# Attention's end: three of the last unit's four tiles by squares and transfers, in place of two

## The chip, the cores and the metric

The kernel runs on one core of a Trainium2 chip. A core has five engines that work side by side and are kept in step by semaphores only: PE (matmul), ACT, DVE, POOL and SP, which does nothing here but issue transfers. The metric is the time of one execution on the device in microseconds, the median of three: 640.15 (639.71 to 640.76).

## The reference, cut to what matters

4096 tokens of 128 values go through three steps, each with a layer norm in front: a mixture-of-experts feed-forward (8 experts, the best 2 per token, and a shared one), an attention over 4096 stored keys and values, and the same feed-forward again.

```python
x = x + 0.5 * ffn(layernorm(x))
x = x + attn(layernorm(x))      # the part that counts here
x = x + 0.5 * ffn(layernorm(x))

q = h @ Wq.T + bq
scores = einsum('bshd,hmd->bshm', q, memory_keys) / sqrt(128)
probs = softmax(scores)
out = einsum('bshm,hmd->bshd', probs, memory_values) @ Wo.T + bo
```

Everything is in 32-bit floats; the kernel splits the operands of the large products into a high and a low part and adds three products.

## The kernel before, in words

The tokens form 8 groups of 512 (four tiles of 128). The attention takes a group against half of the keys (2048) at a time: a **unit**. There are 16 units, 0 to 15; `LAST` is 15.

A unit has 8 half tiles of scores. For each of them PE multiplies (L1488 to L1490), DVE takes the maximum (L1205), and ACT takes the exponentials. The product with the values needs these exponentials with the keys on the partitions, so each 128x128 block has to be turned. There are two ways:

- **By PE** (an "own" tile): ACT writes the exponentials in plain rows (L852), PE transposes each block into PSUM (L1508), ACT copies the high part (`own_high`, L802), and DVE takes the low part (`own_low`, L1193).
- **By squares and transfers** (a "moved" tile): ACT writes the exponentials as 32x32 squares (L843), DVE turns each square in place (`transpose_squares`, L1200, twice per tile), and transfers carry the squares to their place in `probsT` (`move_strip`, L383). ACT then takes the high part (`moved_high`, L818) and POOL the low part (`moved_low`, L608).

`moved_tiles(w)` says how many of the four tiles go the second way: 3 (`MOVED`) in units 1 to 14, and 2 in unit 0 and unit 15.

The keys of a unit are taken in 8 **pairs** of blocks (`UP`). For each pair there are the transposes of the own tiles on PE (`transpose_pair`), `own_high` and `own_low` of what they wrote, `moved_high` and `moved_low` of the moved tiles, and six products with the values (`values`, L1529 to L1531). One PSUM bank, `TB`, holds the transposes, so those of the next pair wait until `own_low` has read the last ones (`p_lo_done`). PE has the order: transposes of pair r+2, then values of pair r.

What follows the order of the work:

- Every engine has its own order, written out by one loop over half steps H = 8u + h. In the last unit's tail (H from 127) ACT does in each half step: `own_high` of a pair, then `moved_high` of the pair behind it. DVE does `own_low` and pieces of other work: maxima, the normalizing L989, and the 16 steps of the routing for the second feed-forward (`route_group`, four per half step, between two `own_low`).
- Pair 0 of a unit can't have its `moved_high` before that unit's transfers are down (`moved[0]`, `moved[1]`): `moved[0]` counts the first two tiles, `moved[1]` the third.
- The transfers of a unit from 3 on are in two batches (`BATCHES`). SP issues batch 0, two tiles in 16 issues of 128 KB, after the squares of both tiles. Then it issues batch 1, the third tile, in 12 issues of 64 KB; the last 4 of batch 1 are issued by ACT, at h = 7, behind the unit's last exponentials (L918 to L924). SP works its list in order.
- In the tail ACT also copies for the second feed-forward: L796 waits for nothing but PE's transposes and stands between `moved_high` of the last unit's pair 0 and its `own_high`. PE's gate products (L1282) wait for that copy and stand in front of the transposes of pair 1.
- POOL has, between the `moved_low` of the last unit's pairs 2 and 3, the addition of a block (L624, L629) and three small operations (L510, L511, L513). The copy L867 on ACT, which stands in front of `own_high` of pair 3, waits for the addition.

Of the kernel before, what the change touches and what calls it, by code (L numbers as in the profile page):

```python
# [35 lines left out]
UNITS = 2 * GROUPS  # L36
# [5 lines left out]
LAST = UNITS - 1  # L42


MOVED = 3
# [11 lines left out]
HALVES = 2 * GT  # L57
# [3 lines left out]
SINGLE = 2  # L61
# [42 lines left out]
def macaron_kernel(nc: bass.Bass, x, wup, wdown, gate_w, expert_bias, shared_up, shared_down,  # L104
                   wq, bq, wo, bo, keys_values, out):
    with ExitStack() as ctx:
# [186 lines left out]
        def wait(eng, s, n):  # L293

            if not isinstance(n, int) or n > 0:
                eng.wait_ge(s, n)
# [31 lines left out]
        def early_logits(i):  # L328

            return (TB, banks[:, 3, :], banks[:, 1, :])[i][:, 0:P]  # L330

        def moved_tiles(w):

            return 2 if w in (0, LAST) else MOVED

        def moved_pair(w, m):

# [20 lines left out]

        def moves(k, units):

            later = max(0, (units if k == 0 else min(units, LAST)) - SINGLE - 1)
            return MOVE * ((min(units, 1) if k == 0 else 0) + later)

        def squares_of(units):
            return 2 * sum(moved_tiles(w) for w in range(units))
# [15 lines left out]
        def move_strip(eng, u, k, tile, count, b, i):  # L381
            done = single[u - 1][tile] if 0 < u <= SINGLE else moved[k]
            eng.dma_start(*strip(u, tile, count, b, i)).then_inc(done, 16)  # L383
# [7 lines left out]
        def pair_at(H):  # L391

            return pairs_until(H) if pairs_until(H + 1) > pairs_until(H) else None

        def projection_at(H):

            w = H // HALVES - 2
            if w < 0 or w >= LAST:
                return None
            return w if H % HALVES == (FIRST_LAG if w == 0 else LAG + 1) else None  # L400
# [269 lines left out]
        def _(act):  # L670
# [25 lines left out]
            def exp_logits(G, logits):  # L696

                act.wait_ge(logits_done, G + 1)
                if G >= 2:
                    act.wait_ge(expz_turned, route_event(G - 2) + 1)  # L700
                act.activation(early_rows if G == GROUPS else expz_rows[:, G % 2, :], logits, ACT.Exp, scale=-1.0).then_inc(expz_done, 1)
# [16 lines left out]
            def copy_wbc(G, bank):  # L718
                act.wait_ge(wbc_done, G + 1)
                wait(act, weighted, (G - 1) * SLOTS)  # L720

                act.activation(wbc[:, G % 2, :].rearrange("p (t a q) -> p t a q", t=GT, a=GT),
                               bank.rearrange("p (a t q) -> p t a q", a=GT, t=GT), ACT.Copy).then_inc(wbc_copied, 1)
# [51 lines left out]
            def copy_xT_for_q(g, bank):  # L775

                act.wait_ge(xT_done, g + 1 + ATTENTION_LN)
                wait(act, q_projected, g)
                act.wait_ge(shared_up_done, GROUPS - AHEAD)
                act.wait_ge(xTb_done, GROUPS - AHEAD)  # L780
                act.activation(xq[:, :], bank, ACT.Copy).then_inc(xT_copied, 1)

            def q_high(g, bank):

                act.wait_ge(q_projected, g + 1)
                wait(act, scores_done, BANKS * GT * 2 * (g - 1))
                act.activation(q_hi[:, g % 2, :], bank, ACT.Identity, bias=bq_scaled[:, 0:1]).then_inc(q_hi_done, 1)

            def early_copy(i, bank):

                if i == 0:
                    act.wait_ge(q_projected, GROUPS)
                else:
                    act.wait_ge(probsT_done, UP * LAST)
                act.wait_ge(xT_done, SECOND_LN + i + 1)
                act.activation(xT[i], bank, ACT.Copy).then_inc(xT_copied, 1)  # L796

            def own_high(ring):

                act.wait_ge(probsT_done, ring + 1)  # L800
                wait(act, pv_done, 2 * (ring - HI_RING + 1))
                act.activation(own_part(p_hi, ring), own_squares(ring), ACT.Copy).then_inc(p_hi_done, 1)  # L802
# [54 lines left out]
            def copy_oT(w):  # L857

                act.wait_ge(pv_done, (w + 1) * KC)
                wait(act, out_proj_done, w)  # L860
                act.activation(oT[:, :], OB, ACT.Copy).then_inc(oT_copied, 1)

            def copy_y(w):

                act.wait_ge(out_proj_done, w + 1)
                wait(act, block_added, w)
                act.activation(y[:, :, :].rearrange("p t d -> p (t d)"), projection_bank(w), ACT.Copy  # L867
                               ).then_inc(y_copied, 1)

            def shift_exponentials(g):  # L870

                act.wait_ge(shift_done, g + 1)
                act.activation(shift_exp[:, :, :].rearrange("p b t -> p (b t)"),
                               shift[:, :, :].rearrange("p b t -> p (b t)"), ACT.Exp).then_inc(shift_exp_done, 1)
# [4 lines left out]
            for u in range(UNITS + 2):  # L879
                g = u // 2  # L880
                prepares = u % 2 == 1 and u < LAST
                for h in range(HALVES):
                    H = u * HALVES + h
                    w = projection_at(H + 3)
                    if u <= LAST and w:
                        copy_oT(w)
                    if projection_at(H + 2) == 0:
                        copy_oT(0)
                    if u == LAST + 2 and h == LAG - 2:
                        copy_oT(LAST)  # L890
                    if u == LAST + 1 and h == 3:
                        early_copy(1, banks[:, 1, :])
                    if u == LAST + 1 and h == 5:
                        exp_logits(GROUPS + 1, early_logits(1))
                        early_copy(2, banks[:, 0, :])
                    if u == LAST + 1 and h == 7:
                        exp_logits(GROUPS + 2, early_logits(2))
                    if u == LAST + 2 and h == 3:
                        copy_wbc(GROUPS, banks[:, 2, :])

                    ring = pair_at(H + 3)
                    if ring is not None:
                        own_high(ring)

                    if u > LAST and w is not None:
                        copy_oT(w)
                    if u < UNITS:
                        exponentials(u, h // 2, h % 2)
                    if u == 0 and h == 6:
                        for done in moved_first[:QUADS * QUADS // 2]:  # L910
                            act.wait_ge(done, 16)
                    of, at_h = divmod(H - 4, HALVES)
                    if 1 <= of <= SINGLE and at_h in (0, 2, 4):
                        tile = at_h // 2
                        wait(act, moved_lo_done, UP * (of - 1))
                        act.wait_ge(squares_done, squares_of(of) + 2 * (tile + 1))
                        if of == 1 and tile == MOVED - 1:
                            act.wait_ge(probsT_done, UP)  # L918
                        for i in range(QUADS):
                            move_strip(act, of, 0, tile, 1, QUADS - 1, i)  # L920
                    if SINGLE < u < LAST and h == HALVES - 1:
                        wait(act, moved_lo_done, UP * (u - 1))
                        act.wait_ge(squares_done, squares_of(u) + 2 * MOVED)
                        for i in range(QUADS):  # L924
                            move_strip(act, u, 1, MOVED - 1, 1, QUADS - 1, i)
                    if prepares and h == Q_HALF - 2:
                        copy_xT_for_q(g + 1, TB)
                    if prepares and h == Q_HALF - 1:
                        q_high(g + 1, TB)
                    if u == LAST and h == Q_HALF - 2:  # L930
                        early_copy(0, TB)
                    if u == LAST and h == Q_HALF - 1:
                        exp_logits(GROUPS, early_logits(0))

                    ring = pair_at(H + 4)
                    if ring == 1:
                        moved_high(0)
                    if ring:
                        moved_high(ring)
                    w = projection_at(H + 2)  # L940
                    if w is not None:
                        copy_y(w)
                    if 2 <= u and u % 2 == 0 and h == 1:
                        shift_exponentials(g - 1)
# [722 lines left out]
```

## Time and profile before

| | |
|---|---|
| median of three runs | 640.15 us (639.71 to 640.76) |
| the profiled execution | 640.2 us, span 638.4 us |
| busy share of the span | PE 94%, DVE 82%, ACT 71%, POOL 65% |
| granted PE clock | full in all 40 slices |
| chain that ended last | PE 65%, DVE 24%, issue 4%, ACT 3% |
| `moved_low` (L608) | 128 of them, 226.9 us of POOL |
| squares (L1200) | 92 of them, 113.5 us of DVE |

The rows shown further down are of these kinds. A row of the chain of waits gives the start, the time in the chain and the work that the end was waiting for. A row of the timeline gives the start, the busy time, engine, line, operation and shapes; x2 stands for two in a row, and the brackets say how long the engine stood idle before and what released it. SPq and ACTq are the queues in which these engines issue transfers. A row of a group gives count, total busy time and the mean in ns. The attention's last scores are at about 514 us, its last products with the values end at about 550.6, and then the second feed-forward runs to the end.

### The profile page before, as it was taken

To read this page: it belongs to the slowest core of one execution; us is meant where nothing else is said; L and a number is where in the kernel's file an instruction comes from. 1 tells how busy PE (TensorE), PEld (TensorE's weight loads), DVE (VectorE), ACT (ScalarE), POOL (GpSimd) and SP (SyncE) were. 2 spreads that over 40 slices of the span, in tenths; PEclk is the share of its full clock that TensorE was granted. 3 is DMA by queue.
4 is the path that set the end of the run, shared out by engine and by line. 5 is a ranking of instruction groups with operands and counts; after the bars stand their busy time and mean duration, and the time that the engine had idled before them with its cause. 6 is when DMAs were issued, how large, how long until landed. Compare 5 with 4: busy or idle time off the path is not lost.

```text
span 638.4 us, 10666 instructions
## 1 busy us (share of the span) xinstructions
PE 597.5 (94%) x3508; PEld 443.3 (69%) x3508; DVE 525.7 (82%) x915; ACT 455.0 (71%) x756; POOL 414.7 (65%) x482
## 2 busy tenths in 40 slices
PE   6798989889899999999999999999999998988987
PEld 2456666567687787777778777787787766655655
DVE  5989886988978978978988897887888858688775
ACT  3577776566777767777777777776876775578886
POOL 3977880564486875966767687596677787645420
PEclk9999999999999999999999999999999999999999
DMA  8012110425447265363643726527355350000000
GB/s 309 13 34 67 37 64 1 128 62 129 112 100 173 55 169 116 84 166 85 147 113 86 178 69 150 128 71 171 91 136 118 82 134 0 1 2 34 35 33 34
DMA packets 36118, 59.28 MB, mean 93 GB/s; under 512 B 9312, under 2 KB 9952, under 8 KB 35936
## 3 DMA queue, kind: packets, MB, share of 16 engines
q1 hardware_dynamic: 31808, 52.82, 32.7%
q10 hardware_dynamic: 3744, 4.74, 2.9%
q0 software_dynamic: 512, 1.05, 0.6%
q8 instruction: 28, 0.46, 0.3%
q14 instruction: 26, 0.21, 0.1%
HBM read 8.25 MB, written 2.10 MB: 16 GB/s over the span
## 4 chain that ended last, share of the span: by engine, by line
PE 65%; DVE 24%; issue 4%; ACT 3%; SPq 1%; DMA 1%; POOL 1%; ACTq 0%; DVEq 0%; POOLq 0%
PE banks L1488 8%; PE banks L1489 7%; PE banks L1490 7%; PE banks L1529 7%; PE banks L1531 7%; PE banks L1530 7%; DVE probsT L1096 6%; PE banks L1508 4%; DVE bank_max L1205 4%; PE banks L1345 4%; DVE E L1200 3%; PE banks L1330 3%; PE banks L1539 2%; PE banks L1361 2%; PE banks L1358 2%
## 5 line engine op out<-in xcount | busy, mean ns | idle before, releaser
L608 POOL TENSOR_TENSOR p_lo<-probsT,p_hi 128x768 fp32r<-128x768 f32 (+1 forms) x128 | 226.9, 1776 | 120.8 <-ACT p_hi L818 120.2
L1205 DVE TENSOR_REDUCE bank_max<-banks 128x1 f32<-128x1024 f32 x128 | 155.9, 1219 | 30.6 <-PE banks L1490 29.8
L818 ACT ACTIVATE p_hi<-probsT 128x768 fp32r<-128x768 f32 (+1 forms) x128 | 104.4, 816 | 29.0 <-PE banks L1531 26.6
L1096 DVE SCALAR_TENSOR_TENSOR probsT<-banks,E 128x1024 bf16<-128x1024 f32 x80 | 95.4, 1216 | 24.7 <-PE banks L1330 24.7
L1488 PE MATMUL banks<-kv_lo,q_parts 128*128 128x512 f32 x256 | 111.6, 436 | 4.1 <-ACT E L843 1.9
L1200 DVE STREAM_TRANSPOSE E<-E 128x1024 f32<-128x1024 f32 x92 | 113.5, 1234 | 0.3 <-ACT E L843 0.2
L843 ACT ACTIVATE E<-banks,neg_max 128x1024 f32<-128x1024 f32 x92 | 102.4, 1113 | 9.7 <-DVE neg_max L1211 8.0
L1529 PE MATMUL banks<-p_hi,kv_lo 128*128 128x512 f32 x256 | 107.7, 421 | 1.7 <-issue 1.7
L716 ACT ACTIVATE probsT<-probsT 128x1024 bf16<-128x1024 bf16 x96 | 92.4, 981 | 16.7 <-DVE probsT L1096 12.4
L1530 PE MATMUL banks<-p_lo,kv_hi 128*128 128x512 f32 x256 | 102.3, 399 | 0.0
L1531 PE MATMUL banks<-p_hi,kv_hi 128*128 128x512 f32 x256 | 102.3, 399 | 0.0
L1489 PE MATMUL banks<-kv_hi,q_parts 128*128 128x512 f32 x256 | 101.4, 396 | 0.0
L1490 PE MATMUL banks<-kv_hi,q_parts 128*128 128x512 f32 x256 | 101.0, 394 | 0.0
L802 ACT ACTIVATE p_hi<-banks 128x256 fp32r<-128x256 f32 (+1 forms) x128 | 52.3, 408 | 62.4 <-PE banks L1508 62.1
L1193 DVE TENSOR_TENSOR p_lo<-banks,p_hi 128x256 fp32r<-128x256 f32 (+1 forms) x128 | 56.1, 438 | 32.4 <-ACT p_hi L802 32.1
L1345 PEld LDWEIGHTS banks<-wdown_b,probsT 128*128 128x128 bf16 x704 | 42.5, 98 | 30.8 <-ACT probsT L716 21.7
L1345 PE MATMUL banks<-wdown_b,probsT 128*128 128x128 bf16 x704 | 52.8, 220 | 7.9 <-ACT probsT L716 7.9
L1529 PEld LDWEIGHTS banks<-p_hi,kv_lo 128*128 128x128 f32 x256 | 48.3, 189 | 14.0 <-issue 4.0
L1330 PE MATMUL banks<-E,wup_b 128*128 128x512 bf16 x176 | 50.8, 381 | 7.3 <-DVE probsT L1096 6.3
L1488 PEld LDWEIGHTS banks<-kv_lo,q_parts 128*128 128x128 f32 x256 | 48.3, 189 | 12.8 <-ACT E L843 3.4
L1531 PEld LDWEIGHTS banks<-p_hi,kv_hi 128*128 128x128 f32 x256 | 48.1, 188 | 12.3
L1530 PEld LDWEIGHTS banks<-p_lo,kv_hi 128*128 128x128 f32 x256 | 48.2, 188 | 11.7 <-issue 1.7
(133 smaller groups left out, 928.3 us busy)
## 6 DMA issues: line engine op xcount, KB each, us to landing
probsT<-E SPq DMA_DIRECT2D x208, 128.0 KB, 2.4
probsT<-E SPq DMA_DIRECT2D x232, 64.0 KB, 2.0
probsT<-E ACTq DMA_DIRECT2D x72, 64.0 KB, 2.1
E<-in_keys_values SPq DMA_DIRECT2D x8, 512.0 KB, 3.6
out<-X SPq DMA_DIRECT2D x8, 256.0 KB, 2.0
X<-in_x SPq DMA_DIRECT2D x1, 1280.0 KB, 9.3
probsT<-E POOLq DMA_DIRECT2D x16, 64.0 KB, 2.4
X<-in_x SPq DMA_DIRECT2D x3, 256.0 KB, 5.5
```

Of the source, the lines that this page charges most:

```text
L608: pool.tensor_tensor(moved_part(p_lo, ring), moved_pair(ring // UP, ring % UP), moved_part(p_hi, ring).bitcast(fp32), ALU.subtract).then_i ...
L818: act.activation(moved_part(p_hi, ring), moved_pair(ring // UP, ring % UP), ACT.Copy).then_inc(moved_hi_done, 1)
L1096: dve.scalar_tensor_tensor(hidden[:, k, :, :], up_banks[PAIR_BANK[k]], 0.0, spread.unsqueeze(1).to_broadcast([P, 2, N]), ALU.max, ALU.mult ...
L1200: dve.transpose(half, half).then_inc(squares_done, 1)
L1205: dve.tensor_reduce(bank_max[:, i % 2, h:h + 1], score_pair(u, i, h).rearrange("p b n -> p (b n)"), AX.X, ALU.max).then_inc(bank_max_done, 1)
L1345: last = pe.matmul(result_banks[G % 2][:, t * D:(t + 1) * D], hidden[:, k, c % 2, t * P:(t + 1) * P], wdown_b[:, c, :], start=(c == 0 and ...
L1488: pe.matmul(bank, qh, kl, start=True, stop=False)
L1489: pe.matmul(bank, ql, kh, start=False, stop=False)
L1490: pe.matmul(bank, qh, kh, start=False, stop=True).then_inc(scores_done, 1)
L1529: pe.matmul(OB, vl, hi, start=(c == 0), stop=False)
L1530: pe.matmul(OB, vh, lo, start=False, stop=False)
L1531: pe.matmul(OB, vh, hi, start=False, stop=(c == KC - 1)).then_inc(pv_done, 1)
```

## The change

Unit 15 now has three moved tiles, like the units in front of it. Its third tile gets two more squares on DVE, 12 more issues on SP and 4 more on ACT; its PE transposes fall from four to two per pair, `own_high` and `own_low` from 512 to 256 columns, and `moved_high` and `moved_low` grow from 512 to 768. The thresholds of `moved[1]` follow.

```diff
         def moved_tiles(w):
 
-            return 2 if w in (0, LAST) else MOVED
+            return 2 if w == 0 else MOVED
...
         def moves(k, units):
 
-            later = max(0, (units if k == 0 else min(units, LAST)) - SINGLE - 1)
+            later = max(0, units - SINGLE - 1)
...
-                    if SINGLE < u < LAST and h == HALVES - 1:
+                    if SINGLE < u < UNITS and h == HALVES - 1:
                         wait(act, moved_lo_done, UP * (u - 1))
                         act.wait_ge(squares_done, squares_of(u) + 2 * MOVED)
                         for i in range(QUADS):
```

On SP, at the end of its list: the two batches of unit 14, batch 0 of unit 15 and the stores of the output before

```order
L383 DMA probsT<-E 32x2x512 x16
L383 DMA probsT<-E 32x512 x12
L383 DMA probsT<-E 32x2x512 x16
L462 DMA out<-X 128x512 x8
L106 UNCONDITIONAL_BRANCH
```

and now:

```order
L383 DMA probsT<-E 32x2x512 x16
L383 DMA probsT<-E 32x512 x12
L383 DMA probsT<-E 32x2x512 x16
L383 DMA probsT<-E 32x512 x12
L462 DMA out<-X 128x512 x8
L106 UNCONDITIONAL_BRANCH
```

Twelve issues are new behind the 16 of unit 15; nothing else moved.

On ACT, from the last exponentials of unit 15 (L852) over `own_high` (L802) and `moved_high` (L818) of unit 14's last pairs to pair 0 of unit 15, before

```order
L852 ACTIVATE probs,row_sum<-banks,neg_max 128x1024
L818 ACTIVATE p_hi<-probsT 128x768
L802 ACTIVATE p_hi<-banks 128x256
L818 ACTIVATE p_hi<-probsT 128x768
L802 ACTIVATE p_hi<-banks 128x256
L818 ACTIVATE p_hi<-probsT 128x768
L873 ACTIVATE shift_exp<-shift 128x8
L802 ACTIVATE p_hi<-banks 128x256
L818 ACTIVATE p_hi<-probsT 128x512
L796 ACTIVATE probs<-banks 128x512
L802 ACTIVATE p_hi<-banks 128x512
```

and now:

```order
L852 ACTIVATE probs,row_sum<-banks,neg_max 128x1024
L383 DMA probsT<-E 32x512 x4
L818 ACTIVATE p_hi<-probsT 128x768
L802 ACTIVATE p_hi<-banks 128x256
L818 ACTIVATE p_hi<-probsT 128x768
L802 ACTIVATE p_hi<-banks 128x256
L818 ACTIVATE p_hi<-probsT 128x768
L873 ACTIVATE shift_exp<-shift 128x8
L802 ACTIVATE p_hi<-banks 128x256
L818 ACTIVATE p_hi<-probsT 128x768
L796 ACTIVATE probs<-banks 128x512
L802 ACTIVATE p_hi<-banks 128x256
```

The four issues stand in front of three `moved_high`; the last two `moved_high` and `own_high` of the piece have their new widths.

On DVE, around the last maxima of unit 15 (L1205), the difference has two squares (L1200) more, each in front of an `own_low` (L1193) of unit 14:

```order
 L1193 TENSOR_TENSOR p_lo<-banks,p_hi 128x256
 L1205 TENSOR_REDUCE bank_max<-banks 128x1
-L1193 TENSOR_TENSOR p_lo<-banks,p_hi 128x256
-L1205 TENSOR_REDUCE bank_max<-banks 128x1
-L1211 TENSOR_REDUCE neg_max<-bank_max 128x1
+L1200 STREAM_TRANSPOSE E<-E 128x4x256
+L1193 TENSOR_TENSOR p_lo<-banks,p_hi 128x256
+L1205 TENSOR_REDUCE bank_max<-banks 128x1
+L1211 TENSOR_REDUCE neg_max<-bank_max 128x1
+L1200 STREAM_TRANSPOSE E<-E 128x4x256
```

Both squares are of unit 15's third tile; the work behind each moves back by one place and keeps its order.

## Rows read from the trace of the kernel before

**Rows 1.** The chain of waits: start, time in the chain, what it was.

```profile
526.32 0.63 PE banks L1508 x4
...
534.90 1.27 POOL X L629
...
544.20 0.24 PE banks L1529
```

**Rows 2.** A window of the tail: busy us (instructions) of each engine, clock, DMA share, GB/s.

```profile
526.30:550.60 24.30, 21.55 (x125) 16.08 (x125) 19.16 (x40) 12.30 (x23) 16.99 (x18) 1.00 0.00 1
```

**Rows 3.** Timeline of the SP queue: issues of units 14 and 15.

```profile
494.02 1.52 SPq L383 DMA_DIRECT2D probsT<-E  x1
...
502.57 0.59 SPq L383 DMA_DIRECT2D probsT<-E  x1
...
510.18 0.63 SPq L383 DMA_DIRECT2D probsT<-E  x1
...
519.51 1.24 SPq L383 DMA_DIRECT2D probsT<-E  x2
```

**Rows 4.** Issues by size: KB each, median us from issue to landing.

```profile
probsT<-E SPq DMA_DIRECT2D x12, 64.0 KB, 2.0
```

**Rows 5.** Groups by line and shape, 505 to 552 us: busy us, mean ns.

```profile
L1200 DVE STREAM_TRANSPOSE E<-E 128x1024 f32<-128x1024 f32 x2 | 2.5, 1234 | 0.0
```

**Rows 6.** Timeline of DVE, then of ACT, 517 to 527 us.

```profile
517.05 0.42 DVE L1193 TENSOR_TENSOR p_lo<-banks,p_hi 128x256 fp32r<-128x256 f32 x1 [1.02 <-ACT p_hi L802]
...
526.22 0.63 ACT L818 ACTIVATE p_hi<-probsT 128x512 fp32r<-128x512 f32 x1 [0.50 <-PE banks L1531]
526.76 0.58 ACT L796 ACTIVATE probs<-banks 128x512 f32<-128x512 f32 x1
```

**Rows 7.** Timeline of ACT behind its four issues of unit 14.

```profile
497.13 0.85 ACT L818 ACTIVATE p_hi<-probsT 128x768 fp32r<-128x768 f32 x1 [1.65 <-PE banks L1531]
```

**Rows 8.** Timeline of PE: gate products, first transposes of pairs, first feed-forward product.

```profile
528.30 0.43 PE L1282 MATMUL banks<-probs,gate_s 128*32 128x128 f32 x8
...
529.23 0.33 PE L1508 MATMUL banks<-ident,E 128*128 128x128 f32 x1
...
538.22 0.30 PE L1508 MATMUL banks<-ident,E 128*128 128x128 f32 x1
...
550.59 0.60 PE L1330 MATMUL banks<-E,wup_b 128*128 128x512 bf16 x2
```

**Rows 9.** Groups by line and shape, 505 to 552 us.

```profile
L608 POOL TENSOR_TENSOR p_lo<-probsT,p_hi 128x768 fp32r<-128x768 f32 x8 | 14.7, 1839 | 4.1 <-ACT p_hi L818 4.0
L608 POOL TENSOR_TENSOR p_lo<-probsT,p_hi 128x512 fp32r<-128x512 f32 x8 | 10.3, 1291 | 6.5 <-ACT p_hi L818 6.5
...
L1193 DVE TENSOR_TENSOR p_lo<-banks,p_hi 128x512 fp32r<-128x512 f32 x8 | 5.5, 685 | 2.4 <-ACT p_hi L802 2.4
L802 ACT ACTIVATE p_hi<-banks 128x512 fp32r<-128x512 f32 x8 | 4.8, 598 | 2.5 <-PE banks L1508 2.5
...
L1193 DVE TENSOR_TENSOR p_lo<-banks,p_hi 128x256 fp32r<-128x256 f32 x8 | 3.3, 416 | 6.0 <-ACT p_hi L802 6.0
L802 ACT ACTIVATE p_hi<-banks 128x256 fp32r<-128x256 f32 x8 | 3.0, 379 | 2.6 <-PE banks L1508 2.6
```

**Rows 10.** Timeline of DVE (normalizing, a routing step), then of POOL's `moved_low`.

```profile
524.71 0.33 DVE L989 TENSOR_SCALAR xn<-X,neg_mean,rstd 128x128 f32<-128x128 f32 x1
...
526.09 1.25 DVE L989 TENSOR_SCALAR xn<-X,neg_mean,rstd 128x128 f32<-128x128 f32 x1
527.26 1.31 DVE L989 TENSOR_SCALAR xn<-X,neg_mean,rstd 128x128 f32<-128x128 f32 x1
...
539.19 0.95 DVE L1038 TENSOR_TENSOR route<-route,best 128x64 f32<-128x64 f32 x1
...
525.43 1.82 POOL L608 TENSOR_TENSOR p_lo<-probsT,p_hi 128x768 fp32r<-128x768 f32 x1 [0.72 <-ACT p_hi L818]
...
537.54 2.52 POOL L608 TENSOR_TENSOR p_lo<-probsT,p_hi 128x512 fp32r<-128x512 f32 x2
```

## The prediction, made before the changed kernel was run

> **Names.** Unit 15 is the last of the 16 attention units. Its exponentials are turned in eight pairs; P0 to P7 are those of unit 15, Q0 to Q7 those of unit 14. Of each pair "T" is its transposes on PE (L1508), "high" and "low" the split of what T wrote (ACT L802, DVE L1193), "moved high" and "moved low" the split of the tiles that came by transfer (ACT L818, POOL L608), "V" its six products (L1529 to L1531).
>
> **What bounds the kernel now.** I read the chain of waits first. In front of 516 us it is PE, product behind product; from there on it changes hands at every pair, between PE, ACT, DVE and POOL: transposes and products of PE, and between them pieces like POOL's addition of a block, 1.27 us [rows 1]. So the stretch from 516 to 550.6, where the second feed-forward starts, is a loop of handovers, and the change lies wholly in it. The windows say the same: PE is at work in 21.55 of 24.30 us there, POOL in 16.99, at a granted clock of 1.00 [rows 2]. What ends a wait counts here, not what an engine has to do in sum. The questions are therefore: when do the new transfers land, who stands behind them, and what is on POOL and DVE at the same time.
>
> **The change part by part.**
>
> *The transfers.* For unit 15 the SP queue now has its first 16 issues and 12 more (the ACT queue 4). SP starts the 16 at 510.18 and ends the last at 519.51+1.24 = 520.75 [rows 3]: the queue is issuing without a break, so the 12 can't start before 520.8, although their squares are ready at 517.2. An issue of 64 KB takes 0.59 [rows 3], with the gap 0.63, so the twelfth starts at 520.8+11×0.63 = 527.7. While ACT issues its four, one issue of SP took 1.52 instead of 0.59 in unit 14 [rows 3]: 0.93 more, 528.7. It lands 2.0 later [rows 4]: 530.7. Without that stretching it would be 529.8; with both queues slow, 531.2.
>
> *The two squares on DVE.* 1.23 each [rows 5]. The second goes in front of the low of Q3 (517.05), ahead of which DVE idled 1.02 [rows 6]: it ends near 517.2, 0.15 after the old start of that low. The first stands in the same place one step earlier, in front of the low of Q2. I cost both at nothing; without that idle time it would be 2.5.
>
> *ACT's four issues.* In unit 14 ACT stood idle 1.65 behind them [rows 7]. Here they stand ahead of the moved high of Q5, and behind it queue the high of Q5 and of Q6: I work out 0.9 for T of Q6, and, since the normalizing on DVE then meets POOL's next moved low, which it had just missed, some 2.4 for T of P0 (526.32 [rows 1] to 528.7). All of this ends before the next wait and is swallowed by it.
>
> *The moved high of P0* waits for the landing: 530.7 in place of 526.22 [rows 6]. ACT works in order, so behind it stand the copy L796, the high of P0 and so on. The copy starts 0.75 later (0.85 [rows 7] less the tenth by which the next one overlaps) and takes 0.58 [rows 6]: 532.05. PE's next work, the gate products, waits for it; they go from 528.30 to 532.1, and T of P1, 0.93 behind them, from 529.23 to 533.0 [rows 8]. **Term 1: +3.8.** Covered before this would have cost nothing; that V of P0 only comes behind T of P2 is no cover, since the wait blocks ACT, not only V.
>
> *From T of P1 to T of P4* (529.23 to 538.22, 8.99 us [rows 8]). The chain runs V of Q7, copy, moved high of P2, moved low of P2, POOL's two operations of the block, the copy L867, high and low of P3. The moved high takes 0.85 for 0.63 [rows 6, 7], the moved low 1.84 for 1.29, the high 0.38 for 0.60, the low 0.42 for 0.69 [rows 9], and two transposes less of the four that take 0.63 [rows 1] give 0.2. Sum +0.2+0.55−0.2−0.25−0.2 = +0.1. But the last of these, T of P4, also had the gate products in front of it: I take 0. T of P4: 542.0. **Term 2: 0** (−0.3 to +0.3).
>
> *From T of P4 to the first feed-forward product* (538.22 to 550.59, 12.37 us [rows 8]). Two things pull. PE has 4×0.2 less, high and low are 0.5 shorter per pair. But POOL has the moved lows of P3 to P5 in a row from 541.9 (537.54 [rows 10], plus the 3.8, plus 0.55 for the longer moved low of P2), 1.8 each, to 543.7, 545.5 and 547.3. And an operation of DVE that has its inputs in SBUF alone doesn't run beside such a POOL operation: the normalizing begun at 526.09 lasted to 527.34, as POOL's moved low 525.43+1.82 ended at 527.25, and the next one, begun at 527.26, met the following moved low and took 1.31, though one that met none took 0.33. A routing step begun at 539.19 lasted 0.95, until the second of the two moved lows from 537.54 was over, at 540.06 [rows 10]. So DVE gets one such operation per POOL operation while POOL works without a gap. Between the lows of P3 and P4 stand four steps of the routing: the first just slips in at 541.75, the second is a reduction and free, the third waits to 543.7, the fourth to 545.5. The low of P4 so starts at 545.55, and T of P5 at 546.0. Its high is done at 546.85, but DVE's next routing step waits to 547.3 and two more follow: the low of P5 ends at 548.3, T of P6 starts at 548.35. From there PE has no wait: T and V (0.2 and six products at 0.24 to 0.25 [rows 1], 1.5), the transposes of the weights (0.45) and T of P7 (0.2) up to 550.7, and three V, 4.5: 555.1 to 555.2 at the first product of the feed-forward, +4.5 against 550.59. Less the 3.8 that stood at T of P4: **Term 3: +0.7.** The same working, done on the old order, comes out 0.2 late there, so I take off 0.2 of the sum.
>
> Bounds of term 3: if DVE never waited for POOL, the end would be POOL's five moved lows, 541.9+5×1.8+1.5 = 552.4: −2.0 against term 1+2, in all +1.8. If the first routing step too comes behind POOL's moved low (541.75 and 541.9 are as good as one moment), one more 1.8 goes by, of which 1.2 remain: +5.5.
>
> The Trainium skill, "SBUF — State Buffer", section "Who interferes with whom", says that a VectorE instruction with two SBUF inputs contends with a GpSimd instruction that reads SBUF, a tensor_scalar can too, and whichever comes first holds the port for its whole duration, while the other blocks. The three DVE rows just named agree, with 1.25, 1.31 and 0.95 us. By a view in which the two only share bandwidth, the change would end near the +1.8; by the rule it is the +4.3.
>
> *Behind the stretch* PE, ACT and DVE pass the same work on in the same order and all start late together. POOL's last moved low, of P7, ends at about 553.0 by this schedule, which is some 5 us later than before; its normalizing behind it slips 0.7 more than PE does, and if nothing covers that, it is inside the upper bound. I see no slack on PE that would give anything back. Nothing in front of unit 15 changes, only thresholds.
>
> **Sum.** +3.8+0+0.7−0.2 = +4.3. The profiled execution took 640.2 with a span of 638.4; the median is 640.15, the same within 0.1. So 644.4.
>
> **The rivals.**
>
> *A. Late, but DVE isn't held up* (+0.6 to +2.5: 640.8 to 642.6). The landing as above, but the routing steps fall into gaps of POOL. For: in the old tail only one in two of these steps was caught. Against: there POOL was idle a third of the time [rows 2], and now its moved lows come without gaps.
>
> *B. The transfers are in time and the shorter pairs win* (−2.5 to −1: 637.6 to 639.1). The queue would have to be done by 526.2. PE saves 8×0.2 and each pair's high and low 0.5; with no wait and no lock this is what the same schedule gives. Against it: 28 issues at 0.63 in a row are 17.7 us, and from 510.18 they can't be out before 527.7. The Trainium skill, "DMA: Bandwidth & Descriptors", section "Issuing engines are not separate DMA queues", says that the time to initiate is usually small against the transfer. By that B would be right; the rows show the opposite here, 0.59 to 0.62 per issue and a queue that never rests. With the transfers in time but POOL in DVE's way it would be +1 to +2.5, which is A's range.
>
> *C. More than I count* (+5.7 to +8: 646 to 648). PE has nothing to do between V of Q6 and the gate products at 532.1, 1.5 to 3.9 us, the longest gap of the attention. The trace of before has a clock of 1.00 in every stretch and so can't price a fall; half the clock for three pairs would be 4.5 us. The Trainium skill, "TensorE: Matmul & The Clock Gate", section "Why this matters for your kernels", warns that an idle PE falls back to its lower clock; no row of before shows it.
>
> **How the numbers follow.** Forecast (+3.2 to +5.6) 0.66; A 0.18; B 0.05; C 0.07; the rest, that a wait nearby gives all of it back and nothing is to be seen, 0.04. What a measurement of this kernel tells from no change is about 0.2%, 1.3 us. Faster by more than that: B, 0.04. Within it: a third of A, the rest, a bit of B, 0.11. Slower: 0.85. Range 641.6 to 646.2, which leaves out B, the low third of A and C; the forecast's own is 643.3 to 645.8.
>
> **What would show it.** In the profile of after: SP's last issue for unit 15 starts near 528.7; the moved high of P0 starts near 530.7 and names the transfer as its releaser; the gate products near 532.1; T of P1 near 533.0 and of P4 near 542.0; between the lows of P3 and P4 two routing steps of over 1 us each; the first feed-forward product near 555. Wrong would be: the moved high of P0 released by PE as before, or routing steps of 0.2 to 0.3 throughout with a first product near 552.

## The result, and the profile after

The changed kernel takes 645.68 us in the median of four runs (645.04 to 647.29), the kernel before 640.14 on the same chip (639.71 to 640.76): 1.0091 of it, with an interval of 1.0077 to 1.0105. It is slower, as forecast; the forecast was 644.4, 1.3 less than this.

The profiled execution of after is its slowest, 647.29 with a span of 645.5. About 1.1 us of that lies outside the changed stretch: TensorE's granted clock was 0.66 in a stretch near 165 us, where the profile of before has 1.00, and 0.8 of the 1.1 arises there. So from here on times in the tail are counted from T of Q3 (516.16 before, 517.24 after). Of all that is different only the two new squares start before it, and they don't delay it: the queue's first issue for unit 15 starts 5.98 before T of Q3 in both profiles. From T of Q3 to the first feed-forward product it was 34.43 us before and is 40.46 now, +6.03. The 1.1 and the 6.03 are all of the 7.1 by which the span grew, so nothing behind the stretch gives time back.

First the late transfers. The chain of waits of after (start, time in the chain, what it was) now runs along the SP queue:

```profile
511.26 0.63 SPq L383
...
521.22 0.64 SPq L383
521.90 0.61 SPq L383
...
527.07 1.25 SPq L383
528.37 0.59 SPq L383
529.00 0.59 SPq L383
529.63 1.99 DMA probsT<-E
```

The 16 issues of batch 0 start at 511.26, and the twelve new ones follow at 521.90 without a rest. The last issue starts at 529.63 and lands at 531.62. Set against [rows 3], SP works 28 issues in 18.96 us, and nothing but its own length holds it up. In the timeline of ACT (in brackets the idle time ahead and its releaser) the first row is the moved high behind ACT's four issues, and the third is the wait for the landing:

```profile
522.27 0.84 ACT L818 ACTIVATE p_hi<-probsT 128x768 fp32r<-128x768 f32 x1 [0.92 <-PE banks L1531]
...
526.65 0.36 ACT L802 ACTIVATE p_hi<-banks 128x256 fp32r<-128x256 f32 x1
531.70 0.84 ACT L818 ACTIVATE p_hi<-probsT 128x768 fp32r<-128x768 f32 x1 [4.69 <-DMA probsT<-E]
532.45 0.58 ACT L796 ACTIVATE probs<-banks 128x512 f32<-128x512 f32 x1
```

The moved high of P0 is released by a transfer; before it was PE [rows 6]. It starts 14.46 behind T of Q3, in place of 10.06. The copy stands behind it, and PE waits for the copy. PE's timeline, answering [rows 1] and [rows 8]:

```profile
517.24 0.44 PE L1508 MATMUL banks<-ident,probs 128*128 128x128 f32 x2 [0.69 <-ACT attended L867]
...
529.15 0.41 PE L1508 MATMUL banks<-ident,probs 128*128 128x128 f32 x2 [1.75 <-DVE p_lo L1193]
529.32 0.48 PE L1529 MATMUL banks<-p_hi,kv_lo 128*128 128x512 f32 x1
...
533.08 0.43 PE L1282 MATMUL banks<-probs,gate_s 128*32 128x128 f32 x8 [2.10 <-ACT probs L796]
...
533.93 0.38 PE L1508 MATMUL banks<-ident,probs 128*128 128x128 f32 x2
534.07 0.61 PE L1529 MATMUL banks<-p_hi,kv_lo 128*128 128x512 f32 x1
...
544.00 0.41 PE L1508 MATMUL banks<-ident,probs 128*128 128x128 f32 x2
...
547.91 0.69 PE L1508 MATMUL banks<-ident,probs 128*128 128x128 f32 x2 [2.08 <-DVE p_lo L1193]
548.25 0.77 PE L1529 MATMUL banks<-p_hi,kv_lo 128*128 128x512 f32 x1
...
557.70 0.60 PE L1330 MATMUL banks<-E,wup_b 128*128 128x512 bf16 x2
```

The rows of L1508 are T of Q3, of P0, of P1, of P4 and of P5; the others are the gate products, the first feed-forward product, and the first product of the V that comes behind T of P0 (V of Q6), behind T of P1 (V of Q7) and behind T of P5 (V of P3). T of P1 is 3.62 later than before, T of P4 4.70, T of P5 5.77 and the last 6.03. V of Q7 and of P3 begin with products of 0.61 and 0.77 where V of Q6 has 0.48: that is the clock. The windows of after (busy us and instructions of PE, PEld, DVE, ACT and POOL, clock, DMA share, GB/s) show where, against 1.00 in [rows 2]:

```profile
516.16:528.00 11.84, 9.69 (x48) 6.97 (x46) 8.31 (x21) 8.02 (x16) 9.52 (x7) 1.00 0.80 187
528.00:535.00 7.00, 3.75 (x25) 2.75 (x26) 3.15 (x7) 2.72 (x5) 2.97 (x3) 0.95 0.16 40
535.00:545.00 10.00, 7.87 (x43) 5.55 (x42) 8.42 (x20) 5.25 (x11) 7.80 (x8) 0.87 0.00 0
545.00:556.00 11.00, 8.92 (x37) 6.90 (x36) 9.27 (x13) 3.95 (x7) 8.10 (x6) 0.84 0.00 0
```

The products at the lower level start one per 0.43 us, at the higher one per 0.24: 1.2 GHz for 2.4. The six of V of Q7 take 2.5 instead of 1.43, so the first fall costs 1.1. The second, behind the 2.08 of waiting in front of T of P5, costs 0.9: from T of P5 to the first feed-forward product it is 9.79, and 8.91 in the profile of fill (below), whose clock stayed up. Between T of P4 and of P5 stands the other wait. The timelines of DVE and POOL of after, answering [rows 10]:

```profile
525.14 3.54 DVE L989 TENSOR_SCALAR xn<-X,neg_mean,rstd 128x128 f32<-128x128 f32 x2
...
543.43 0.42 DVE L1193 TENSOR_TENSOR p_lo<-banks,p_hi 128x256 fp32r<-128x256 f32 x1
543.77 0.21 DVE L1074 SCALAR_TENSOR_TENSOR route<-route 128x64 f32<-128x64 f32 x1
544.02 0.22 DVE L1036 TENSOR_REDUCE best<-route 128x8 f32<-128x64 f32 x1
544.27 1.49 DVE L1038 TENSOR_TENSOR route<-route,best 128x64 f32<-128x64 f32 x1
545.79 1.73 DVE L1041 TENSOR_TENSOR route<-route,rank 128x64 f32<-128x64 f32 x1
547.45 0.41 DVE L1193 TENSOR_TENSOR p_lo<-banks,p_hi 128x256 fp32r<-128x256 f32 x1
```

```profile
543.81 5.40 POOL L608 TENSOR_TENSOR p_lo<-probsT,p_hi 128x768 fp32r<-128x768 f32 x3
```

While POOL does three moved lows without a gap, from 543.81 to 549.21, the first routing step slips in just ahead, the reduction is free, and each of the next two lasts until one of POOL's operations ends.

### The profile page after: what moved, and what is told of

It is laid out like the page before. It is cut to its first block, busy times and chain, and to the rows that moved or that the text cites. A ratio compares the mean times of both kernels' runs of the same rounds, so it can differ in the third digit from the quotient of the medians.

```text
span 645.5 us, 10653 instructions
## 1 busy us (share of the span) xinstructions
PE 599.0 (93%) x3492; PEld 444.6 (69%) x3492; DVE 533.1 (83%) x917; ACT 453.9 (70%) x756; POOL 418.9 (65%) x482
## 3 DMA queue, kind: packets, MB, share of 16 engines
q0 software_dynamic: 512, 1.05, 0.6%
## 4 chain that ended last, share of the span: by engine, by line
PE 62%; DVE 25%; issue 4%; SPq 4%; ACT 3%; DMA 1%; ACTq 0%; POOL 0%; DVEq 0%; POOLq 0%
PE banks L1488 7%; PE banks L1489 7%; PE banks L1490 7%; PE banks L1529 7%; PE banks L1531 7%; PE banks L1530 7%; DVE probsT L1096 5%; DVE bank_max L1205 5%; DVE E L1200 4%; PE banks L1345 4%; PE banks L1508 4%; SPq L383 4%; PE banks L1330 3%; PE banks L1539 2%; PE banks L1361 2%
## 5 line engine op out<-in xcount | busy, mean ns | idle before, releaser
L608 POOL TENSOR_TENSOR p_lo<-probsT,p_hi 128x768 fp32r<-128x768 f32 (+1 forms) x128 | 231.3, 1812 | 124.6 <-ACT p_hi L818 124.1
L1205 DVE TENSOR_REDUCE bank_max<-banks 128x1 f32<-128x1024 f32 x128 | 155.9, 1218 | 31.1 <-PE banks L1490 30.3
L818 ACT ACTIVATE p_hi<-probsT 128x768 fp32r<-128x768 f32 (+1 forms) x128 | 106.1, 829 | 32.8 <-PE banks L1531 25.2
L1200 DVE STREAM_TRANSPOSE E<-E 128x1024 f32<-128x1024 f32 x94 | 116.0, 1234 | 0.6 <-ACT E L843 0.6
L843 ACT ACTIVATE E<-banks,neg_max 128x1024 f32<-128x1024 f32 x94 | 104.5, 1112 | 9.9 <-DVE neg_max L1211 8.5
L802 ACT ACTIVATE p_hi<-banks 128x256 fp32r<-128x256 f32 (+1 forms) x128 | 50.4, 394 | 64.3 <-PE banks L1508 64.3
L1193 DVE TENSOR_TENSOR p_lo<-banks,p_hi 128x256 fp32r<-128x256 f32 (+1 forms) x128 | 53.9, 421 | 31.7 <-ACT p_hi L802 31.4
L1508 PE MATMUL banks<-ident,probs 128*128 128x128 f32 x256 | 51.5, 280 | 8.6 <-DVE p_lo L1193 7.0
```

The source lines that it names most:

```text
L608: pool.tensor_tensor(moved_part(p_lo, ring), moved_pair(ring // UP, ring % UP), moved_part(p_hi, ring).bitcast(fp32), ALU.subtract).then_i ...
L818: act.activation(moved_part(p_hi, ring), moved_pair(ring // UP, ring % UP), ACT.Copy).then_inc(moved_hi_done, 1)
L1200: dve.transpose(half, half).then_inc(squares_done, 1)
L1205: dve.tensor_reduce(bank_max[:, i % 2, h:h + 1], score_pair(u, i, h).rearrange("p b n -> p (b n)"), AX.X, ALU.max).then_inc(bank_max_done, 1)
```

## The experiments

One table first, for all kernels: how far behind T of Q3 four rows of PE stand in the profile of each, then the median of its runs and the ratio to the kernel before, run beside it on the same chip. Three chips were used for the experiments, with medians of before of 639.98 (no_sp to fill), 640.28 (psum_before to psum_split) and 640.88 (the last two); so medians of different groups compare only within some tenths. 

| kernel | T of P1 | T of P4 | T of P5 | feed-forward | against before | median us | ratio, interval |
|---|---|---|---|---|---|---|---|
| before | 13.07 | 22.06 | 24.90 | 34.43 | | 640.15 | |
| after | 16.69 | 26.76 | 30.67 | 40.46 | +6.03 | 645.68 | 1.0091, 1.0077–1.0105 |
| no_sp | 14.59 | 23.57 | 27.48 | 37.39 | +2.96 | 643.06 | 1.0044, 1.0032–1.0056 |
| no_third | 13.70 | 22.70 | 26.62 | 35.53 | +1.10 | 641.75 | 1.0027, 1.0018–1.0037 |
| late_only | 17.55 | 27.73 | 30.59 | 40.11 | +5.68 | 645.22 | 1.0083, 1.0066–1.0099 |
| fill | 16.90 | 25.90 | 29.86 | 38.77 | +4.34 | 645.02 | 1.0080, 1.0067–1.0093 |
| psum_before | 13.07 | 22.06 | 24.10 | 33.23 | −1.20 | 639.26 | 0.9978, 0.9965–0.9990 |
| psum_after | 17.72 | 26.72 | 28.40 | 38.07 | +3.64 | 644.03 | 1.0052, 1.0033–1.0071 |
| split | 15.21 | 24.20 | 28.11 | 37.89 | +3.46 | 643.42 | 1.0049, 1.0034–1.0063 |
| psum_split | 15.14 | 24.14 | 25.81 | 35.47 | +1.04 | 641.56 | 1.0014, 1.0000–1.0028 |
| after_again | 17.19 | 27.10 | 31.01 | 39.93 | +5.50 | 644.72 | 1.0070, 1.0048–1.0093 |
| fill_again | 17.67 | 26.66 | 30.61 | 39.52 | +5.09 | 645.02 | 1.0065, 1.0043–1.0087 |

**no_sp**: after without SP's twelve issues, so that part of the third tile's data is old.

```diff
...
-                    if first >= moved_tiles(u):
+                    if first >= moved_tiles(u) or (u == LAST and k == 1):
```

> The changed kernel without SP's 12 issues for the third tile of the last unit (its squares on DVE and ACT's 4 issues stay; the moved high of pair P0 waits for those 4 only, so part of that tile's data is old). Theory (landing late, then POOL in DVE's way, then PE's clock): the moved high of P0 no longer waits for a transfer, PE's clock stays at 1.00, and what is left is ACT's issues and the held-up routing steps: +2.6 against the kernel before, 642.7. Rival 1 (the wider pairs on POOL cost all of it, the transfers nothing): as the changed kernel, 645 to 646. Rival 2 (with the transfers in time the shorter pairs win): 637.6 to 639.1.

Without them the moved high of P0 is released by PE again, in the ACT timeline of no_sp:

```profile
526.82 0.84 ACT L818 ACTIVATE p_hi<-probsT 128x768 fp32r<-128x768 f32 x1 [0.50 <-PE banks L1531]
```

and in its PE timeline T of P0 comes 11.98 behind T of Q3, where before it was 10.16:

```profile
528.45 0.41 PE L1508 MATMUL banks<-ident,probs 128*128 128x128 f32 x2 [1.75 <-DVE p_lo L1193]
```

The twelve issues are half of the loss: 2.6 of 5.5 us by the medians (a ratio of 1.0044 for 1.0091), 3.1 of 6.0 by the profiles. The slip of T of P0 that the late landing had swallowed is laid bare, 1.8 of it. 1.0 of what stays is a fall of the clock: its windows give 0.84 from 545 to 556, and T of P5 to the first feed-forward product is 9.91 for the 8.91 of fill.

**no_third**: also without ACT's four issues; only the wider splits, the fewer transposes and the two squares are left, and all of the third tile's data is old.

```diff
...
-                    if SINGLE < u < UNITS and h == HALVES - 1:
+                    if SINGLE < u < LAST and h == HALVES - 1:
```

> The changed kernel without any of the 16 issues for the third tile of the last unit (the squares stay; part of the data is old). Theory: with ACT's four issues gone too, T of P0 comes as before, and only POOL in DVE's way is left: +1.1, 641.2; the step from the kernel without SP's issues (1.5) is ACT's four issues. Rival 1: 645 to 646. Rival 2 (DVE isn't held up): 637.6.

T of P0 is at 10.35, its old place but for 0.2, so the slip was ACT's four issues, and the squares cost nothing. The end is at +1.10, and a hold-up of that size arises where term 3 said, between T of P4 and of P5 (3.92 for 2.84). There is a second one that the forecast didn't have: T of P1 is 0.63 late, since PE waits 0.67 in front of it for the normalizing, which was held up too (two operations in 3.03); the shorter pairs give these 0.6 back behind T of P5. The wider shape, for which the transfers are made, is itself a loss of 1.1 in the profile and 1.6 in the median.

**late_only**: pairs as before, with four transposes and splits of 512, but the transfers of the third tile are made and unit 15 waits for them.

```diff
+            return 2 if w in (0, LAST) else MOVED
+
+        def sent_tiles(w):
+
             return 2 if w == 0 else MOVED
...
-                    if first >= moved_tiles(u):
+                    if first >= sent_tiles(u):
...
```

> The third tile of the last unit is turned by squares and sent in all 16 issues, and the moved high of P0 waits for it, but the pairs of the last unit have the widths of before: two moved tiles, two by PE's transposes (of squares instead of rows, so part of the data is wrong). This is the late landing alone. Theory: the lateness is nearly all of the change's cost and the widths cancel: moved high of P0 near 530.7 to 531.7, then the old pairs, +4 to +5 with a fall of PE's clock in it: 644.1 to 645.2. Rival 1 (the wider pairs cost it): 640.2 to 641. A third possibility, that the wider pairs win something even here: this kernel slower than the changed one, 646 or more.

Lateness alone costs what the whole change costs, 645.22 against 645.68. The ACT timeline of late_only has the same wait:

```profile
530.93 0.63 ACT L822 ACTIVATE p_hi<-probsT 128x512 fp32r<-128x512 f32 x1 [5.26 <-DMA probsT<-E]
```

T of P4 to T of P5 is 2.86 here, so the hold-up is gone with the shape. Of its +5.68, 4.48 stand at T of P1, with a landing 0.7 later than in after, and 1.19 more come up to T of P4; its clock was 0.83 from 528 to 535 and 0.95 up to 545. So its +5.68 and the +1.10 of no_third don't add up to the +6.03 of after, and the sum can't be read finer.

**fill**: after with 20 products whose result nobody uses, in PE's waits in front of T of P0, the gate products and T of P5.

```diff
...
+                    if u == LAST + 1 and h in (4, 5):
+                        pe.wait_ge(exp_done, 2 * GT * UNITS)
+                        fill(6 if h == 4 else 7)
+                    if u == LAST + 2 and h == 1:
+                        pe.wait_ge(y_copied, LAST)
+                        fill(7)
```

> The changed kernel with 20 products that nobody reads on PE, 6, 7 and 7 in the three waits of the tail (in front of T of P0, of the gate products, of T of P5), of 0.24 us each, shorter than the waits. Theory (the fall of PE's clock comes from these waits and costs 1 to 1.7 us): clock 1.00 in all windows of the tail, values products at 0.24 throughout, 644.0 to 644.6. Rival (the fall costs nothing, since PE waits anyway): 645.3 to 645.8. If the products themselves are in the way: above 646.

The windows of fill, against those of after above:

```profile
528.00:535.00 7.00, 5.45 (x33) 3.73 (x31) 3.19 (x6) 3.58 (x7) 3.61 (x2) 1.00 0.11 27
535.00:545.00 10.00, 8.38 (x47) 6.19 (x47) 9.48 (x20) 5.36 (x11) 9.29 (x9) 1.00 0.00 0
545.00:556.00 11.00, 10.31 (x48) 7.13 (x48) 8.96 (x17) 3.82 (x7) 7.40 (x7) 1.00 0.00 0
```

With work in the waits the clock stays at 1.00, and the tail is the one that I had worked out: T of P1 +3.83, T of P1 to P4 9.00 (8.99 before), T of P5 +4.96, the end +4.34. So the waits let it fall, as far as two profiles can say (that of fill_again is the other). But they don't bring the fall each time: psum_after (below) has waits of 1.73 and 3.19 in the same two places, and its clock is 1.00 in all of the tail. Its PE timeline and its window say:

```profile
533.21 0.43 PE L1287 MATMUL banks<-probs,gate_s 128*32 128x128 f32 x8 [3.19 <-ACT probs L800]
```

```profile
528.00:535.00 7.00, 3.61 (x26) 2.67 (x27) 2.07 (x6) 2.72 (x5) 2.25 (x2) 1.00 0.13 30
```

The Trainium skill, "TensorE: Matmul & The Clock Gate", section "Why this matters for your kernels", warns that long idle gaps between products bring the clock down. The trace of after agrees in kind, with a fall behind waits of 1.75 and 2.10 and one pair's work between; that of psum_after doesn't. In time the filler shows little: the median, 645.02, lies above the 644.0 to 644.6 of the theory and is only 0.66 under after's, and the intervals overlap.

**psum_before, psum_after**: the last routing's intermediate tiles lie in PSUM in place of SBUF, so that each comparison has one input there; once on the kernel before, once on after.

```diff
+            if G == GROUPS:
+                return tuple(route[:, a, 0:T, :] if a == 4 else
+                             banks[:, 4, a * T * E:(a + 1) * T * E].rearrange("p (t e) -> p t e", e=E)
+                             for a in range(6))
...
```

> The kernel before (two moved tiles in the last unit), with the five of the six arrays of the second feed-forward's first routing in a free PSUM bank, so that none of its steps has two inputs in SBUF. Nothing else changes. Theory (a routing step waits only because it meets POOL's operation in SBUF): L1064, L1038 and L1045 go from 0.6 to 1.2 down to 0.2 to 0.4 us beside POOL's moved lows, and the tail is 1.4 shorter: 638.6. Rival (the steps were long for another reason, or PSUM makes every step slower): 640.0 to 640.6.

> The changed kernel with the same routing in PSUM. Theory: the landing stays late (T of P1 +3.8), but the low of P4 no longer stands behind two held-up steps, T of P5 comes 2.5 earlier, and the first feed-forward product is at +1.5 to +1.8 with the clock at full speed; with a fall of the clock in the wait for the transfer +1 more: 641.7 to 643.0. Rival (the held-up steps were no bound, POOL's own three moved lows in a row are): 644 to 645.7.

The DVE timeline of psum_before:

```profile
538.28 0.23 DVE L1042 TENSOR_TENSOR banks<-banks,best 128x64 f32<-128x64 f32 x1
538.55 0.23 DVE L1045 TENSOR_TENSOR banks<-banks,rank 128x64 f32<-128x64 f32 x1
```

and its POOL timeline:

```profile
537.33 2.51 POOL L612 TENSOR_TENSOR p_lo<-probsT,p_hi 128x512 fp32r<-128x512 f32 x2
```

The first of the DVE rows is the step that took 0.95 in [rows 10]. Now it and the next take 0.23 each while POOL's moved lows run. T of P4 to T of P5 falls from 2.84 to 2.04, the tail by 1.20, and the kernel is 639.26, the fastest here. In psum_after the two steps of 1.49 and 1.73 take 0.23 each, and T of P4 to T of P5 falls from 3.91 to 1.68: two inputs in SBUF were the hold-up, and not the operation. But I had expected all of it to come through, and only part did: 644.03 lies where the rival (POOL's own moved lows are the bound) had put it. The chain of waits of psum_after shows what is late next:

```profile
542.90 6.46 POOL p_lo L612 x4
549.37 1.38 issue
550.74 2.02 POOL p_lo L612
```

POOL's five moved lows, the bound named under term 3, now set the end; POOL's own timeline has all five without a gap, in 9.88 us, so the 1.38 is a part of them. And its transfers landed 3.70 us after the last issue, not 1.99, in the same view:

```profile
528.06 3.70 DMA probsT<-E
```

That puts T of P1 1.0 later than in after, in a profile with a clock of 1.00.

**split**: for unit 15 alone, batch 0 is the first tile in issues of 64 KB, and batch 1 the other two in issues of 128 KB, so that the queue can start one tile of squares earlier.

```diff
+        def batches(u):
+            return ((0, 1), (1, 2)) if u == LAST else BATCHES
...
```

The rest of the edit makes ACT's four issues 128 KB as well and lets a late copy of DVE (L1005 of after) wait for the second batch; that copy starts at 546.79, some 20 us behind the last issue, so this wait costs nothing.

> The changed kernel with other batches for the last unit: its first tile goes alone in 16 issues of 64 KB as soon as its squares are done (SP stands idle there for some 7 us), and the second and third together in 12 issues of SP and 4 of ACT of 128 KB. Theory: SP starts the 12 at about 517.3 instead of 520.8 and the last lands near 527.6, 3 us earlier; then ACT's four issues bind (T of P0 +2.4) and the held-up steps: +2.6, 642.6, without or with less of a fall of the clock. Rival (the landing isn't what the change costs): 645 to 646.

The moved high of P0 starts 12.98 behind T of Q3, between before's 10.06 and after's 14.46. Its ACT timeline names PE as releaser:

```profile
529.51 0.84 ACT L821 ACTIVATE p_hi<-probsT 128x768 fp32r<-128x768 f32 x1 [3.23 <-PE banks L1535]
```

But that is a product of V of Q6, which happened to end then; in no_sp the same moved high starts ahead of V of Q6 and needs nothing of it. What ended at that moment is the transfers: SP's last issue starts at 525.2, and the last ones land 4.0 to 4.2 us after their issue. The window of split suggests why they took longer than the 2.0 of after, though no run tests it; the DMA engines are full:

```profile
523.00:527.00 4.00, 3.50 (x16) 2.52 (x16) 3.05 (x4) 1.88 (x5) 3.97 (x3) 1.00 1.05 234
```

In psum_split (below), with the same transfers, the view names them. Its ACT timeline:

```profile
527.82 0.84 ACT L825 ACTIVATE p_hi<-probsT 128x768 fp32r<-128x768 f32 x1 [3.16 <-DMA probsT<-E]
```

So the queue is out 3.7 us earlier than in after (8.7 behind T of Q3 in place of 12.4), but the landing comes only 1.5 earlier and still binds: T of P1 is at +2.14, where ACT's issues alone leave +1.5 (no_sp). The theory's landing of 2 us behind the issue didn't hold. In the median split is 2.3 under after, 643.42 where 642.6 was expected. The hold-up stays, and there is a fall of the clock in its +3.46: its window from 545 to 556 gives 0.84, and T of P5 to the first feed-forward product is 9.78 for the 8.91 of fill.

**psum_split**: split with the tiles in PSUM.

> Both: the batches of the last unit as in the kernel before this one, and the routing in PSUM. Theory: T of P1 +2.0, then nothing held up, and the shorter pairs count: -0.2, 639.8, so three moved tiles are then no worse than two with the old routing, but worse than two with the routing in PSUM (638.6). Rival (the two effects don't add up, since one covers the other): 641.5 or more.

The two gains add up against after (−2.3 and −1.7 in the medians, −4.1 together; −2.6, −2.4 and −5.0 in the tail), so the rival's reason, that one covers the other, is wrong. But they leave +1.04 in the tail and 641.56 in the median, the rival's number, where I had expected to be level with before. T of P1 is still 2.07 late, since the transfers land 4.09 us behind the last issue. So the change can be repaired down to the edge of what can be measured, and not made to pay: the kernel before with PSUM tiles is 2.3 us under it.

**after_again, fill_again**: both once more, on one chip, to see how much profiles of the same kernel differ.

> The changed kernel once more, unchanged, on the same chip as the next one. It was at +5.5 (four executions, 645.04 to 647.29). Theory: 4.3 of it are the landing and the held-up steps, the rest falls of PE's clock in the tail, whose number differs from one execution to the next: +5 to +5.5 in the median, and in each execution a clock under 1.

> The changed kernel with the 20 products that nobody reads in PE's waits, unchanged, beside the changed kernel. Theory (the falls cost time): 0.7 to 1.2 under the changed kernel's median, +4.3 to +4.8 against the kernel before. Rival (the falls cost nothing in the median): the same time as the changed kernel within 0.3.

After's second tail is +5.50 with a clock of 0.76 from 528 to 535 and 1.00 behind; fill's second is +5.09 with 1.00 in all of the tail, but its landing was 1.0 later than in after, 15.44 behind T of Q3. In the medians nothing is between them, 644.72 and 645.02. I had expected a mean clock under 1 in each execution of after: two of these six had 1.00, at 644.60 and 644.84. And after_again's ratio of 1.0070 is well under the 1.0091 of the first four executions. Over both pairs of runs, a mean granted clock of 0.999 or 1.000 is shown by two of the ten executions of after and by eight of the eleven of fill; the medians of the ten and of the eleven are 645.06 and 645.02. So the filler keeps the clock up, and a gain in time from it was not shown.

## Why the prediction was right, point by point

**Right in sign and in its mechanism; low by 1.3 in size.**

*Term 1, +3.8.* Measured +3.62 in after, +3.83 in fill; the repeats have +4.12 (with the clock down from the gate products on) and +4.60 (with the landing 1.0 later), so that a hit within 0.2 is partly luck. The last issue starts 18.37 behind the first (forecast 18.5), and the landing is 1.99 later (2.0). The stretching by ACT's issues looked otherwise than in unit 14: up to 0.06 on each of four issues, and then a single issue of 1.25, begun at 527.07, nearly 5 us after ACT's last. The sum is the same, its working is not; that ACT's issues are what stretches SP's was argued and is not shown.

*ACT's four issues.* Forecast to put T of P0 2.4 later and to be swallowed. It slipped 1.75 in after, 1.8 in no_sp and 0.2 in no_third, and was swallowed in after, whose T of P1 follows from the landing alone. The hold-up of the normalizing by POOL, on which the figure rests, is there (two operations in 3.54, each until one of POOL's moved lows ends). That it also delays T of P1 by 0.6 where the transfers are in time, as in no_third, was not in the working.

*The squares, 0.* Right: no_third has both, and its T of P0 is within 0.2.

*Term 2, 0.* 9.00 in fill against 8.99. In after it is 10.07, all of the difference being V of Q7 at the lower clock.

*Term 3, +0.7.* Its main piece, T of P5 1.2 later relative to T of P4 (546.0 less 542.0, less the 2.84 of before), measured +1.07 in after, +1.12 in fill and +1.08 in no_third, by two steps of 1.49 and 1.73 (forecast: the third and the fourth, the first slipping in, the reduction free). The end in fill is +4.34, forecast +4.3; fill_again, with its later landing, has +5.09. Of the page of the Trainium skill cited there, "SBUF — State Buffer", section "Who interferes with whom", the case now shows both sides: what it says blocks did block, up to POOL's whole operation (1.73 us of its 1.8), and with one input in PSUM it didn't (0.23).

*Which step failed.* Rival C, more than counted, was given 0.07 and nothing of it was in the sum, since the trace of before shows no fall of the clock. The falls came: two in after's profile (1.1 and 0.9 us), one or more in those of after_again, no_sp, late_only and split, none in those of no_third, psum_after and psum_split. The second one of after, as those of no_sp and split, stands behind a third wait, the 2.08 in front of T of P5, which is the hold-up of term 3. I took the wait as one gap and didn't see that the slip of T of P0 that I called swallowed leaves a second gap of 1.75 ahead of it, with one pair's work between them. In the profile the falls are 1.7 of the 6.03 (the difference to fill). Whether it is what the median has above the forecast stays open: fill's medians lie no lower than after's repeat, and the landing, which varied by over 1 us between profiles, is as good a candidate. Six more runs of the changed kernel gave 644.72, 0.3 from the forecast, so part of the 1.3 is the spread of such runs; beside them the kernel before was at 640.88, not 640.14.

*The rivals.* A (DVE not held up) is refuted by the DVE rows of after; its price is near psum_after's, +3.64, not the +1.8 of the lower bound. POOL's five moved lows bound the end there as that bound has it, but they started 0.8 later behind T of Q3 than forecast and took 2.0 each in place of 1.8. B (transfers in time, shorter pairs win) is refuted twice: the transfers were late, and no_third, which has the shorter pairs and waits for none, is slower than before by 1.0027.

## What to carry to other kernels

Before work is moved from an engine to transfers, count the issues of the queue as work of that queue: 28 issues at 0.6 us are a stage of some 18 us (18.96 here) that starts only when its input is ready, and at the end of a program no later unit covers it. If fewer and larger issues are to shorten it, see whether the DMA engines have room: in split the queue was out 3.7 us earlier and the landing came 1.5 earlier. What an in-order engine does behind the wait is late as well, whoever needs it. If short VectorE operations turn long beside GpSimd, put one of their inputs in PSUM before rescheduling anything: it was the only edit here that made the kernel faster (639.26 for 640.28 beside it).

## What the runs showed of the hardware that I had not expected

- TensorE's granted clock fell to its lower level behind two waits of 1.75 and 2.10 us with 1.4 us of products between them, and again behind one of 2.08 (0.95, 0.87 and 0.84 in the windows of after), and stayed at 1.00 in both profiles in which products filled them. But waits alone don't decide it: it also stayed at 1.00 in psum_after, with 1.73 and 3.19 in the same places, and in after_again behind the same 2.08. What tells these profiles apart stays open.
- Also in mid-kernel, at about 165 us, the profile of after has a stretch at a lower clock, as has fill_again's; those of before and the nine other profiles have 1.00 there. The windows of after:

```profile
165.00:170.00 5.00, 5.00 (x17) 3.65 (x16) 4.50 (x11) 3.57 (x7) 3.67 (x2) 0.66 0.50 124
```

- The same last transfer landed 1.99 us after its issue in after, after_again, fill and late_only, and 3.70 and 3.64 in psum_after and fill_again. In the first four one of SP's issues had taken 1.03 to 1.83; in the last two none took over 0.7. In split, with issues of 128 KB back to back and a DMA share of 1.05, the last ones landed 4.0 to 4.2 us after their issue.
- Two normalizing operations of DVE, one alone 0.33 [rows 10], took 3.54 together beside POOL's moved lows.
